# Moving the value projections and three of the exponentials' copies in a fused attention kernel

## The reference, cut to what matters

```python
q, k, v = (split_heads(x @ W + b) for W, b in ((Wq, bq), (Wk, bk), (Wv, bv)))   # 16 heads of 8
scores = q @ k.T / scale                       # scale = sqrt(3 * 8)
scores += (take(q @ pos_k.T, c2p_pos) + take(k @ pos_k.T, p2c_pos).T) / scale
out = softmax(scores) @ v                      # per batch and head, 128 x 128
out = layernorm(out @ Wo + bo + x) * ln_scale + ln_bias
x = layernorm(x + out)
```

## Time and profile before

| what | us |
|---|---|
| median of 3 runs (lowest, highest) | 2737.05 (2734.18, 2737.12) |
| the profiled execution, its time | 2735.33 |
| its span | 2733.6 |
| first unit's exponentials start, last one's start | 70.9, 828.4 |
| busy in the span: PE, DVE, ACT, POOL | 2375.6, 2129.8, 2270.4, 577.6 |

### The profile page before, as it was taken

How to read it: one execution, slowest core, us unless ns; L and a number is a source line. 1 busy time by engine, 2 the same in 40 slices (tenths; PEclk the granted TensorE clock), 3 DMA queues, 4 the chain that set the end, 5 groups by cost and what they waited for, 6 DMA issues and landing times. The chain is left out here.

```text
span 2733.6 us, 64386 instructions
## 1 busy us (share of the span) xinstructions
PE 2375.6 (87%) x18133; PEld 1298.0 (47%) x18133; DVE 2129.8 (78%) x6451; ACT 2270.4 (83%) x4511; POOL 577.6 (21%) x435
## 2 busy tenths in 40 slices
PE   3888888888883478555999999999999999999997
PEld 2666665666662256233444444444444444444443
DVE  4778888788775766954788888888888888888886
ACT  2899999989993533266999999999999999999996
POOL 3233242332420011233111111111111111111114
PEclk6999999999996589876999999999999999999999
DMA  4231222312211000000111111111111111111112
GB/s 112 53 77 44 68 58 51 75 45 67 58 43 46 1 0 0 31 0 1 47 52 57 46 46 46 46 52 57 46 46 46 46 53 56 46 46 46 46 52 87
DMA packets 195627, 129.61 MB, mean 47 GB/s; under 512 B 26667, under 2 KB 184443, under 8 KB 195579
## 3 DMA queue, kind: packets, MB, share of 16 engines
q1 hardware_dynamic: 195579, 129.02, 17.9%
HBM read 78.10 MB, written 4.73 MB: 30 GB/s over the span
## 5 line engine op out<-in xcount | busy, mean ns | idle before, releaser
L2002 DVE TENSOR_TENSOR c_Hl<-c_HF,c_Hh 128x512 f16<-128x512 f32 x1028 | 679.4, 688 | 161.5 <-ACT c_Hh L1889 145.1
L1885 ACT ACTIVATE c_HF<-c_H,c_b 128x512 f32<-128x512 f32 x1028 | 710.6, 691 | 64.2 <-PE c_H L1824 44.0
L1889 ACT ACTIVATE c_Hh<-c_H,c_b 128x512 f16<-128x512 f32 x1028 | 706.2, 687 | 0.0
L1940 POOL TENSOR_TENSOR c_EX<-c_euler,c_D 128x16 f32<-128x16 f32 x65 | 188.7, 2902 | 1194.1 <-DVE c_D L1975 1194.1
L1823 PE MATMUL c_H<-c_Cl,SH 128*128 128x512 f16 x1028 | 390.2, 380 | 0.0
L1822 PE MATMUL c_H<-c_Ch,SH 128*128 128x512 f16 x1028 | 390.2, 380 | 0.0
L1824 PE MATMUL c_H<-c_Ch,SH 128*128 128x512 f16 x1028 | 390.0, 379 | 0.0
L1833 PE MATMUL c_Y<-c_Hh,SH 128*128 128x512 f16 x1024 | 388.1, 379 | 0.1
L1835 PE MATMUL c_Y<-c_Hl,SH 128*128 128x512 f16 x1024 | 388.1, 379 | 0.0
L1834 PE MATMUL c_Y<-c_Hh,SH 128*128 128x512 f16 x1024 | 388.1, 379 | 0.0
L649 ACT ACTIVATE a_E<-a_T,a_nm 128x128 f32<-128x128 f32 x1024 | 325.3, 395 | 27.6 <-DVE a_nm L741 26.2
(11 more groups left out here) (296 smaller groups left out, 4076.2 us busy)
## 6 DMA issues: line engine op xcount, KB each, us to landing
c_CWB<-c_rows SPq DMA_DIRECT2D x260, 256.0 KB, 4.0
a_AB<-a_ST SPq DMA_DIRECT2D x256, 128.0 KB, 2.4
a_QN<-a_QH SPq DMA_DIRECT2D x128, 32.0 KB, 1.9
a_KN<-a_KH SPq DMA_DIRECT2D x128, 32.0 KB, 1.9
out<-d_O SPq DMA_DIRECT2D x16, 256.0 KB, 2.3
a_QN<-a_QL SPq DMA_DIRECT2D x64, 32.0 KB, 1.9
a_KN<-a_KL SPq DMA_DIRECT2D x64, 32.0 KB, 1.9
CUR<-in_ctx SPq DMA_DIRECT2D x1, 1848.0 KB
```

Source lines behind the costliest of these rows:

```text
L1885: act.activation(HF[:, k % 4, :], bH[k % 4][:, :], ACT.Gelu_apprx_tanh, bias=b1[:, g % EXPERTS, f:f + 1], scale=1.0 / WSCALE).then_inc(hf_ ...
L1889: act.activation(Hh[:, g % 2, f, :], bH[k % 4][:, :], ACT.Gelu_apprx_tanh, bias=b1[:, g % EXPERTS, f:f + 1], scale=1.0 / WSCALE).then_inc( ...
L2002: dve.tensor_tensor(Hl[:, g % 2, f, :], HF[:, k % 4, :], Hh[:, g % 2, f, :], ALU.subtract)\
```

## The change

- The value projections go from steps 10 to 13 to steps 20 to 23 of the position part, behind the two chunks of the step and, in step 23, ahead of the four unread matmuls. They write bank bO and no longer bM.
- DVE adds the bias from bO straight into V, in step 1 of the next block (step 14 and tile VN before). The copy on POOL goes, with its semaphore and PE's wait on it.
- ET of units 5, 7 and 9 (steps 8, 10 and 12) is copied by DVE and not by ACT. On DVE the copy stands behind `add_positions` and ahead of `split_rows` of the step. PE waits for whichever engine copied (`columns_done`).
- In step 15 DVE does the first `softmax_outputs` ahead of `add_positions` (behind it before).
- The four unread matmuls write bE[0]. In the preamble a fill of ET on POOL and one matmul on PE go.

```diff
-V_STEPS = (10, 11, 12, 13)
+V_STEPS = (20, 21, 22, 23)
+DVE_ET = (5, 7, 9)
+ACT_ET = tuple(w for w in range(UNITS) if w not in DVE_ET)
...
-            def values_out(i, nxt):
-                if nxt:
-                    hold(pool, spare_pool, pv.sem, pv.at(i, UNITS))
-                hold(pool, spare_pool, vn_ok.sem, vn_ok.at(i, 1 + nxt))
-                pool.tensor_copy(V[:, :, :, 0:DH], VN[:, :, :, :]).then_inc(v_ok.sem, 1)
...
             def project_v(b):
-                pe.matmul(bM[:, b * S:(b + 1) * S], xT[:, :, b], Wv[:, :], start=True, stop=True).then_inc(v_ps.sem, 1)
+                pe.matmul(bO[:, b * S:(b + 1) * S], xT[:, :, b], Wv[:, :], start=True, stop=True).then_inc(v_ps.sem, 1)
...
+            def columns_done(i, w):
+                if w in DVE_ET:
+                    pe.wait_ge(ed_ok.sem, ed_ok.at(i, DVE_ET.index(w) + 1))
+                else:
+                    pe.wait_ge(et_ok.sem, et_ok.at(i, ACT_ET.index(w) + 1))
...
             def exp_transposes(i, w):
...
-                    pe.wait_ge(et_ok.sem, et_ok.at(i, w - 1))
+                    columns_done(i, w - 2)
...
             def weighted_values(i, w):
-                pe.wait_ge(et_ok.sem, et_ok.at(i, w + 1))
+                columns_done(i, w)
...
-                    if u in V_STEPS and not last:
-                        project_v(V_STEPS.index(u))
                     for n in tiles_of(u):
...
                     if u >= UNITS and not last:
                         for c in (2 * (u - UNITS), 2 * (u - UNITS) + 1):
                             position_chunk(i, 1, c)
+                    if u in V_STEPS and not last:
+                        project_v(V_STEPS.index(u))
                     if u == UNITS + TAIL - 1 and not last:
                         for _ in range(4):
-                            pe.matmul(bO[:, :], window[:, 0:P], ...
+                            pe.matmul(bE[0][:, :], window[:, 0:P], ...
...
-                    if 0 <= u - 3 < UNITS:
+                    if u - 3 in ACT_ET:
                         exp_columns(i, u - 3)
...
+            def values_in(i):
+                dve.wait_ge(v_ps.sem, v_ps.at(i, NB))
+                dve.tensor_tensor(V[:, :, :, 0:DH], bO[:, :].rearrange("p (b h d) -> p b h d", b=NB, h=NH),
+                                  bv_all[:, :].rearrange("p (a h d) -> p a h d", a=1, h=NH).to_broadcast([P, NB, NH, DH]),
+                                  ALU.add).then_inc(v_ok.sem, 1)
...
+            def exp_columns(i, w):
+                dve.wait_ge(et_ps.sem, et_ps.at(i, w + 1))
+                dve.wait_ge(pv.sem, pv.at(i, w - 2))
+                dve.tensor_copy(ET[:, w % 3, :, :], bE[w % 2][:, :].rearrange("p (h s) -> p h s", h=HG))\
+                    .then_inc(ed_ok.sem, 1)
...
                 for u in range(UNITS + TAIL):
+                    if u == OUT_NORM[0]:
+                        softmax_outputs(i, 0)
                     if u < UNITS:
                         add_positions(i, u)
-                    for b in range(NB):
+                    for b in range(1, NB):
                         if u == OUT_NORM[b]:
                             softmax_outputs(i, b)
+                    if u - 3 in DVE_ET:
+                        exp_columns(i, u - 3)
                     if u in (2, 3) and not last:
                         low_half(i, 1, u - 2)
-                    if u == 14 and not last:
-                        values_in(i, 1)
+                    if u == 1 and not first:
+                        values_in(i)
```

More of the change, by code:

```diff
@@ L41 @@
 TILE_STEPS = (5, 6, 7, 8, 9, 10, 11, 12)
-V_STEPS = (10, 11, 12, 13)
+V_STEPS = (20, 21, 22, 23)
 C2P_MID, P2C_MID = 47, 17
-CONSTS, FILLS, TAB, BUILT = 13, 6, 10, 4
+CONSTS, FILLS, TAB, BUILT = 13, 5, 10, 4
 DVE_CHUNKS = tuple((c, 1) for c in range(1, CHUNKS))
@@ L164, in attention_stage @@
         POS = sb("POS", [P, 2, ROWX, S])
-        VN = sb("VN", [P, NB, NH, DH])
         V = sb("V", [P, NB, NH, VCOLS])
@@ L206, in attention_stage @@
         tab_ps, tab, built = sem("tab_ps"), sem("tab"), sem("built")
-        xb, xT_ps, xT_ok, vn_ok, v_ok, kd_ok = (
-            Count(sem(n), 1) for n in ("xb", "xT_ps", "xT_ok", "vn_ok", "v_ok", "kd_ok"))
+        xb, xT_ps, xT_ok, v_ok, kd_ok = (Count(sem(n), 1) for n in ("xb", "xT_ps", "xT_ok", "v_ok", "kd_ok"))
         v_ps = Count(sem("v_ps"), NB)
@@ L223, in attention_stage @@
         et_ps = Count(sem("et_ps"), UNITS, credit=3)
-        et_ok = Count(sem("et_ok"), UNITS, credit=2)
+        et_ok = Count(sem("et_ok"), len(ACT_ET), credit=2)
+        ed_ok = Count(sem("ed_ok"), len(DVE_ET))
         pv = Count(sem("pv"), UNITS, credit=3)
@@ L377, in _ @@
             pool.memset(V[:, :, :, DH:DH + 1], 1.0).then_inc(filled, 1)
-            pool.wait_ge(filled, 5)
-            pool.memset(ET[:, 0, :, :], 0.0).then_inc(filled, 1)
             pool.wait_ge(filled, FILLS)
@@ L382, in _ @@
             spread_keys(0, 0)
-            values_out(0, 0)
             def power(i, n):
@@ L407, in body @@
                     spread_keys(i, 1)
-                    values_out(i, 1)
             body(0, first=True)
@@ L490, in out_rows @@
                 if b >= 2:
-                    pe.wait_ge(et_ok.sem, et_ok.at(i, UNITS - 3 + b))
+                    columns_done(i, UNITS - 4 + b)
                 elif not last:
@@ L511, in out_transpose @@
                 pe.wait_ge(on_ok.sem, on_ok.at(i, b + 1))
-                if b == 0 and not last:
-                    pe.wait_ge(vn_ok.sem, vn_ok.at(i, 2))
                 if b == 0 and last:
@@ L550, in _ @@
             pe.wait_ge(filled, FILLS)
-            pe.matmul(bO[:, :], ident[:, :], ET[:, 0, :, :], start=True, stop=True)
             for n in range(TILES):
@@ L588, in body @@
                             position_chunk(i, 1, c)
+                    if u in V_STEPS and not last:
+                        project_v(V_STEPS.index(u))
                     if u == UNITS + TAIL - 1 and not last:
                         for _ in range(4):
-                            pe.matmul(bO[:, :], window[:, 0:P], table[:, 0:2, :, :].rearrange("p g k n -> p (g k n)"),
+                            pe.matmul(bE[0][:, :], window[:, 0:P], table[:, 0:2, :, :].rearrange("p g k n -> p (g k n)"),
                                       start=True, stop=True)
@@ L893, in _ @@
                 low_half(0, 0, k)
-            values_in(0, 0)
+            dve.wait_ge(filled, FILLS)
+            values_in(0)
             dve.wait_ge(built, BUILT)
```

## The result

| | before | after |
|---|---|---|
| median (lowest, highest), us | 2738.76 (2734.18, 2742.29) | 2744.91 (2742.00, 2746.34) |
| profiled execution, its time and span | 2735.33, 2733.6 | 2742.00, 2740.1 |
| period of a steady block (mean of blocks 2 to 13 of 0 to 15) | 48.72 | 49.03 |
| the last unit's exponentials start (the first of their four; 828.4 above is the fourth) | 827.46 | 833.98 |

Both have seven runs. The ratio is 1.0027, with an interval of 1.0018 to 1.0037: slower by 6.2 us, which is little but more than the noise, where 2745.5 was forecast.

What follows compares the result with a forecast made beforehand. ACT, PE and DVE near full, so order decides: ACT in steps 6 to 13, DMAs in step 16, DVE in the position part. Fifteen blocks at +0.59 (+8.9), last block -0.4: profiled 2743.8, plus 1.7 gives 2745.5 us; range 2730 to 2756.

Steps and rivals of the forecast that it cites:

- The copies, -0.58 us a block: Steps 8 to 12: of ACT's 1.44 us relief only 0.58 reach the last split, and so chunk 0.
- the cheap copy: Rival: an ET copy on DVE takes a spacing of 0.30 us, not 0.60; 2741 us, chance 0.08.
- The tail, +1.17 us: Position part: the four value projections of 0.57 us each on PE make the next scores 1.17 us a block later.
- The block's start has no slack: Next block's scores: DVE's last copy would release them at 410.38, PE at 411.16, so the 1.17 us loss counts.
- The net, +0.59 a block: Each block with a successor: -0.58 from the copies and +1.17 from the tail; fifteen of them give +8.9 us.
- The signs: Error tests: last split over 1 us earlier in the block, or chunk 9 to the scores growing by under 0.8 us.
- values_in in step 1: DVE's bias addition, 0.60 us, fits in about 1.4 us of idle time; uncovered it would cost 0.60 a block.
- The last block, -0.4: Without buckets and chunks, the last block gains 0.4 us of ACT's 1.44, PE's step being nearly as long as ACT's.
- the new order: First softmax output ahead of the additions in step 15: valued at 0 while chunk 0 waits for DMAs; could not cost.
- the projections were not swallowed: Rival: PE's waits before the chunks hide the first three projections, tail costs 0.57; net 0 a block, 2737 us, chance 0.14.
- passed in full: Rival: chunk 0 gains all 1.44 us; 2733 us with the tail's cost (chance 0.07), 2724 with it hidden (0.11).
- brought nothing: Rival: the copies only move ACT's wait to DVE, leaving +1.17 a block; 2754.5 us, chance 0.14.

Runs made afterwards that it cites:

- e5: The kernel after with all ET copies back on ACT, plus four semaphore increments ahead of DVE's loop: 1.0035 against the kernel before, period 49.50 us.
- e2: The kernel before with only the three ET copies moved to DVE, projections still in steps 10 to 13: 1.0011 against before, period 49.07 us.
- e6: The kernel before with the ET copies on DVE and projections in steps 4, 9, 11 and 13, ahead of the transposes: 0.9977, period 48.20 us.
- e4: The kernel after without the four unread matmuls at a block's end: 1.0012 against the kernel before, period 48.68 us.
- e10: The kernel after with six unread 384-column matmuls on PE in step 16, in the wait ahead of chunk 0: 1.0017 against the kernel before.
- e1: The kernel after with all ET copies back on ACT, so the value move alone: 1.0293 against the kernel before, 2821.36 us.
- e8: The kernel before, ET copies on DVE, projections in steps 4, 9, 11, 13, and buckets and projections ahead of the transposes: 0.9972, period 47.87 us.

## Why the prediction was right

The replay in detail, in the time of the block of the earlier trace rows (the rows of after less 2.84; before by the earlier trace rows):

| | before | forecast | after |
|---|---|---|---|
| transposes of step 9 | 380.37 | 380.79 | 380.79 |
| ST 4 | 382.25 | 382.16 | 382.15 |
| transposes of step 11 | 384.85 | 384.96 | 384.96 |
| ST 6 | 387.01 | 386.53 | 386.60 |
| last split | 389.77 | 389.19 | 389.27 |
| chunk 0 | 397.51 | 396.93 | 396.98 |
| chunk 12 (forecast 407.38, less the 0.58 gained) | 406.78 | 406.80 | 406.73 |
| chunk 15 (forecast 409.17, likewise) | 408.57 | 408.59 | 408.52 |
| chunk 15 to the next scores | 1.42 | 1.99 | 1.78 |

- *The copies, -0.58 us a block.* Measured -0.53 at chunk 0, with the chain of waits as drawn: 1.58 us from the first addition of step 8 to the transposes (1.57 forecast), the DMAs still last before chunk 0, 7.71 us after the last split. The choice of 0.60 us a copy was right: the next instruction starts 0.60 behind a copy that takes 0.68 (382.89 and 383.49). The Trainium skill, VectorE: DVE Perf Modes, section "Why PSUM operands drop a tier", gives a copy of float32 from PSUM the base rate only; the trace agrees, as the copy takes the 0.68 us of the addition and not half of it, and the cheap copy is refuted. e5 shows the copies' worth on top of the value move, 0.47. What the forecast left unsaid, and e2 and e6 show, is that this needs the projections gone from behind the transposes of steps 10 to 13.
- *The tail, +1.17 us.* Measured 0.48 + 0.36 = 0.84 (0.85 by the period). Up to chunk 15 the replay holds within 0.1: it is 0.48 late against chunk 0, not 0.59 or 0.60. The term that failed is the last. I charged the fourth projection in full, 0.57, though the stretch from chunk 15 to the scores grew by 0.36 only. Of the 1.42 us in the earlier trace rows, part was no work of PE's: from the unread matmuls to the scores 1.08 us passed (408.91 to 409.99), and in the kernel after 0.87. Before, the scores had 0.21 us of waiting for DVE's last copy in them, and a projection fits into that first. (The profile marks no wait there. But in e4, where it marks one, the scores start 0.91 us after that copy does; before, it is 0.96, from 409.03 to 409.99; after, 1.27.) "The block's start has no slack" is the sentence that failed: I had the copy's release at 410.38 for the new block and did not ask what it was for the old. e4 shows the same wait from the other side: with the matmuls gone, PE waits for that copy, and 0.35 us of period is all that they cost.
- *The net, +0.59 a block*, was +0.32, so +4.7 in place of +8.9.
- *The signs.* Neither sign of being wrong came: the last split is 0.50 us earlier in the block, and the stretch from chunk 9 to the scores grew by 0.84, hardly over the 0.8 that I had set. DVE waits for PE 0.18 and 0.26 us before the copies of chunks 10 and 12, as foretold. values_in in step 1, put at 0, cost nothing that e5 shows.
- *The last block, -0.4.* Measured +0.72 up to the last unit's exponentials. The experiments take it apart: this stretch is 25.81 us before, 26.30 in e2, which has the copies alone (+0.49), 26.05 in e5, which has all but the copies (+0.24), and 26.53 after. So the copies, which I had put at a gain, cost half a microsecond here: ACT's exponentials have three new waits for DVE in the last block, 0.64, 0.20 and 0.30 us. The rest fits the softmax output that now stands ahead of the last additions, as the last block has no projections to move; no run has that order alone. I had valued the new order at 0 for blocks where chunk 0 waits for DMAs, and forgot the block that has no chunk 0.
- *Not forecast:* the half-clock stretch in block 0, 1.16 us by e10 (0.92 with block 1).

So 2745.5 came as close to 2744.9 as it did by luck: the fifteen blocks were put 4.2 us too dear, and other things made it up, namely the last block (1.1), block 0's clock (0.9), blocks 1 and 14 (0.4), and a median that stands 2.9 us above the profiled execution where I took 1.7. From median to median the forecast was a rise of 8.5 us, and 6.2 were measured. The direction and the chain of causes were right, and of the rivals none happened: the projections were not swallowed (e5: 0.78 us a block), the copies neither passed in full nor brought nothing, and they were not cheap.

## What to carry to other kernels

Work that is moved to relieve a busy engine has to land in a wait, not in a stage where the receiving engine's order decides. The same four projections made the block 0.32 us longer than before in the position part, and 0.52 shorter in PE's waits for ET, with the same copies on DVE. When a term is added to a stretch between two events, first split the old stretch into work and waiting; the new term eats the waiting first. And when one experiment is out of proportion to its edit, look at the instruction queue before a story is built on it.

## What the runs showed of the hardware that I had not expected

- Where the loop of an engine's program lies can cost more than the edit: e1 lost 4.4 to 4.6 us of DVE at the start of thirteen blocks, with 90 packets on the instruction queue for 25 and 22 half-clock stretches in the attention, and four instructions ahead of the loop took it away (2821.36 us to 2747.86). A comparison of kernels whose instruction counts differ can hide this, as e1's did.
- A half-clock stretch (clock 0.57 over a window of 4.00 us) costs about 1.45 us here (49.70 against 48.20 in blocks of e6, 49.35 against 47.87 of e8). It came in some blocks and not in others of the same code. In the steady blocks of all kernels but e1 it stood behind the wait ahead of chunk 0; in e1 others stand behind DVE's idle time at a block's start. Block 0 or 1 has one in every profile except those of before and e10. What decides when it comes stays open: neither the length of the wait (1.38 us without it in the steady blocks of after, 0.6 with it in one of e6) nor the fill accounts for it.
